# A graph network layer on one core: the vector engine's four products of a block in one run, the selection, the bases and the additions behind them

## The chip, the core and the metric

The kernel runs on one core of a Trainium2 chip. A core has a matrix engine (PE), a vector engine (DVE), a scalar engine (ACT), a general engine (POOL) and a sync engine (SP) that issues DMAs. Each works through its own instruction list in order, and they wait for one another on semaphores. The metric is the device time in microseconds (us) of one launch, the median of several runs.

## What is computed

A message passing layer over 12,500 nodes (128 features) and 412,500 edges that are sorted by their destination, with a residual addition and a layer norm behind it. Cut to what matters:

```
f0, f1   = node features @ W1            # 32 scalars, 32 vectors of 3
h        = gelu(gelu(edge_scalar_attr @ W_mlp1 / sqrt(8)) @ W_mlp2 / sqrt(64))
w00, w01, w10, w11 = h @ Wp_..           # 32 weights each, for every edge
e0, e1   = f0[edge_src], f1[edge_src]    # the gather
messages = w * e * edge_attr             # scalars and vectors, four kinds of product
n0, n1   = segment_sum(messages, edge_dst)
x        = layernorm(x + cos * self(x) + sin * (n0, n1) @ W2)
```

## The kernel before

A setup part builds a feature table in DRAM and the transposed accumulator `acc` in SBUF. The edge loop follows, then the layer norm. The edge loop is where the time is. It goes over 202 blocks of 2,048 edges; a block has 16 tiles of 128 edges, in four chunks of four tiles. The loop's body holds eight blocks (`RING`), one `step(b, ...)` each, and each engine has its own `step`. No scheduler sets the order: the program text of each engine is its order.

What a block needs, engine by engine:

- **POOL** gathers the rows of the feature table of 16 tiles with 16 indirect DMAs (L432) into one of four slots of `gath`. Before it gathers into a slot again it waits until the fourth products of the block four before are done (`s_prod[3]`).
- **PE** runs, for four blocks ahead, the two layers of the small network: layer 1 (L701) and layer 2 (L706), each in two halves, with the gelus of ACT (L513, L518) between them through one PSUM bank. So half 0 of layer 1, its gelu, half 0 of layer 2, its gelu, half 1 of layer 1, and so on form one serial chain. Between them it makes the block's weights, chunk by chunk (`radial`, L716), the segment sums of each chunk (L730), the transposes of these sums (L741) and the convolution with W2 (L749, `y_ps`).
- **DVE** makes the products of each chunk, weights times gathered rows (`products`, L958 once and L961 twice per chunk), the selection of the next block (`select`, L945 and L950: a one-hot by the destination, times the edge attributes), reads the window bases of the last block (`load_bases`, L974), and adds 16 windows of the last block's `y_ps` to `acc` (`add_windows`, L986).
- **ACT** runs the gelus, copies the sums and the transposed sums out of PSUM (L532, L539, L540), copies the indices of a later block (L497) and lays the next block's attributes in PSUM (L528), in the bank in which `y_ps` is too.

Waits that matter here: the products of chunk c wait for its weights (`s_w[c]`), its gathered rows and for PE's segment sum of the same chunk of the block before (`s_seg[c]`). The selection of block b+1 waits for `s_seg[3]` of block b-1 and for the attributes (`s_eap`). The convolution of block b-1 stands on PE in step b between the segment sum of chunk 1 and half 1 of layer 2. It waits for the transposed sums, for the additions of the block before (`s_add[15]`), and for the selection of block b+1 (`pe.wait_ge(s_sel, selected)`, with `selected = b + 2`), because the attributes in the same bank must have been read. The additions wait for the convolution (`s_y`).

## Time and profile before

| | us |
|---|---|
| median of three runs | 5436.78 |
| lowest and highest | 5435.55, 5450.42 |
| the profiled execution | 5456.17 |
| its span | 5454.4 |
| PE busy (matmul) | 3305.5 |
| POOL busy | 3103.3 |
| DVE busy | 1878.1 |
| ACT busy | 1180.1 |

The profiled execution is one of its own, 0.36% above the median. "Busy" counts computing instructions; a PE row's end is modelled, not observed. No engine is busy for more than 61% of the span, so the order of waits sets the time, not one engine's work. The rows further down say which waits ended what: in brackets behind a row stands the idle time of its engine before it, and what ended that.

### The profile page before, as it was taken

Reading aid. Unit: us, or ns where it says so; the run is one execution under the profiler, and the core shown is the slowest. Engines: PE = TensorE matmul, PEld = TensorE weight load, DVE = VectorE, ACT = ScalarE, POOL = GpSimd, SP = SyncE. Lnnn points to the kernel's source line nnn. Section 1 sums busy time; section 2 is a strip of 40 time slices with the busy share of each in tenths; the row PEclk is TensorE's granted clock in tenths of the full one; section 3 lists DMA queues with packets and bytes.
Section 4 is the critical chain, followed back from the end, with each engine's and each line's share of the span. In section 5 each row is a group of like instructions: output and inputs, shape, how many; then the busy total and the mean of one; then the engine's idle time right before and its main releaser. Section 6 shows DMA issues by size and latency. Waiting matters only on the chain.

```text
span 5454.4 us, 53973 instructions
## 1 busy us (share of the span) xinstructions
PE 3305.5 (61%) x15272; PEld 1812.2 (33%) x15272; DVE 1878.1 (34%) x6401; ACT 1180.1 (22%) x2646; POOL 3103.3 (57%) x3281
## 2 busy tenths in 40 slices
PE   5666656665665655666466666565665565666566
PEld 4233333332333323333233333233333333333334
DVE  2233333333333333333233333333333333333335
ACT  2122222221222212222122222121221221222124
POOL 5266566555665556556555665566566565566551
PEclk7677777777777777777777777777777777777777
DMA  6022222121221212212122222122122122222111
GB/s 151 16 46 46 44 46 45 45 44 41 46 46 43 45 41 46 46 43 46 44 42 45 45 46 44 42 47 46 42 46 46 43 46 44 45 46 46 44 44 59
DMA packets 586056, 256.03 MB, mean 47 GB/s; under 512 B 528383, under 2 KB 531867, under 8 KB 584347
## 3 DMA queue, kind: packets, MB, share of 16 engines
q0 software_dynamic: 103616, 211.52, 14.9%
q1 hardware_dynamic: 480572, 42.82, 6.7%
q14 instruction: 160, 1.31, 0.1%
q10 hardware_dynamic: 1696, 0.18, 0.0%
q8 instruction: 12, 0.20, 0.0%
HBM read 241.45 MB, written 12.81 MB: 47 GB/s over the span
## 4 chain that ended last, share of the span: by engine, by line
another core or an unknown queue 47%; PE 28%; issue 15%; ACT 8%; DVE 0%; ACTq 0%; DMA 0%; DVEq 0%; SPq 0%; POOL 0%; POOLq 0%
PE bank L706 7%; PE bank L716 5%; PE bank L701 5%; PE bank L749 5%; PE bank L730 3%; PE bank L741 2%; ACT h L513 2%; ACT big L518 1%; ACT ztsb L539 1%; ACT ztsb L540 1%; ACT bank L528 1%; PE bank L658 1%; ACT big L616 1%; ACT idx L497 1%
## 5 line engine op out<-in xcount | busy, mean ns | idle before, releaser
L432 POOL DMA_INDIRECT gath<-feature_table,idx x3224 | 3077.1, 954 | 2219.8 <-issue 1767.6
L716 PE MATMUL bank<-wpbd,big 128*128 128x256 f32 x3232 | 989.8, 436 | 98.4 <-issue 97.1
L958 DVE TENSOR_TENSOR big<-bank,gath 128x256 f32<-128x256 f32 x808 | 341.6, 423 | 1704.8 <-remote 1461.2
L716 PEld LDWEIGHTS bank<-wpbd,big 128*128 128x128 f32 x3232 | 711.8, 226 | 547.0 <-issue 480.0
L749 PE MATMUL bank<-ztsb,conv 128*128 128x128 f32 x1616 | 350.4, 384 | 788.8 <-ACT ztsb L540 491.2
L961 DVE TENSOR_TENSOR big<-bank,gath 128x384 f32<-128x384 f32 x1616 | 816.9, 547 | 0.0
L741 PE MATMUL bank<-ident,zsb 128*128 128x128 f32 x1616 | 340.1, 349 | 701.4 <-issue 544.6
L706 PE MATMUL bank<-h,w2bd 128*128 128x512 f32 x820 | 578.6, 795 | 259.8 <-ACT h L513 166.1
L986 DVE TENSOR_TENSOR acc<-acc,bank 128x8 f32 x3232 | 527.4, 163 | 598.5 <-remote 106.0
L701 PE MATMUL bank<-e8T,w1bd 128*128 128x512 f32 x820 | 591.9, 811 | 175.1 <-ACT big L518 90.2
L518 ACT ACTIVATE big<-bank 128x512 f32<-128x512 f32 x410 | 449.4, 1096 | 714.3 <-PE bank L706 396.7
L749 PEld LDWEIGHTS bank<-ztsb,conv 128*128 128x128 f32 x1616 | 298.8, 277 | 907.8 <-issue 503.9
L730 PE MATMUL bank<-big,sel 128*32 128x256 f32 x6464 | 596.3, 446 | 5.6 <-DVE big L961 4.9
L741 PEld LDWEIGHTS bank<-ident,zsb 128*128 128x128 f32 x1616 | 256.2, 182 | 963.4 <-issue 782.7
L532 ACT COPY zsb<-bank 128x512 f32<-128x512 f32 x404 | 237.9, 589 | 1106.1 <-remote 982.3
L945 DVE TENSOR_TENSOR sel<-rel_all,bank 128x128 f32<-128x128 f32 (+1 forms) x202 | 58.0, 287 | 1118.4 <-issue 952.0
L513 ACT ACTIVATE h<-bank 128x512 f32<-128x512 f32 x410 | 246.8, 602 | 796.7 <-remote 388.4
L539 ACT COPY ztsb<-bank 128x64 f32<-128x64 f32 x404 | 95.8, 237 | 1390.1 <-remote 1345.5
L701 PEld LDWEIGHTS bank<-e8T,w1bd 128*128 128x128 f32 x820 | 150.1, 229 | 410.8 <-issue 237.4
L706 PEld LDWEIGHTS bank<-h,w2bd 128*128 128x128 f32 x820 | 156.3, 237 | 373.8 <-ACT h L513 194.2
L730 PEld LDWEIGHTS bank<-big,sel 128*32 128x32 f32 x6464 | 136.3, 116 | 285.4 <-issue 285.2
L950 DVE TENSOR_TENSOR sel<-sel,bank 128x512 f32<-128x512 f32 x202 | 138.7, 686 | 6.9
(77 smaller groups left out, 756.2 us busy)
## 6 DMA issues: line engine op xcount, KB each, us to landing
gath<-feature_table,idx POOLq DMA_INDIRECT x3224
e<-in_edge_attr SPq DMA_DIRECT2D x416, 32.0 KB
ea_t<-in_edge_attr SPq DMA_DIRECT2D x100, 64.0 KB
feature_table<-gath SPq DMA_DIRECT2D x4, 1280.0 KB, 5.6
out<-big SPq DMA_DIRECT2D x4, 1280.0 KB
big<-in_x SPq DMA_DIRECT2D x3, 1280.0 KB, 8.5
dst_rows<-in_dst SPq DMA_DIRECT2D x1, 1536.0 KB
big<-in_src SPq DMA_DIRECT2D x1, 1408.0 KB
```

What stands on the lines that cost most here:

```text
L432: pool.indirect_dma_start(out=gath[:, s % SLOTS, t, :], out_offset=None, in_=table[:, :], in_offset=bass.IndirectOffsetOnAxis(ap=idx[:, s, ...
L513: act.activation(h1[:, h, :], hid_ps[:, :], ACT.Gelu_apprx_tanh, scale=1.0 / math.sqrt(RADIAL)).then_inc(s_h1[h], 1)
L518: act.activation(h2[:, m // SUPER % 2, :, :, 2 * (m % SUPER) + h], hid_ps[:, :].rearrange("q (b p) -> q b p", b=SUPER), ACT.Gelu_apprx_tan ...
L701: pe.matmul(hid_ps[:, :], w1bd[:, 2 * (m % SUPER) + h, :], e8T[:, :], start=True, stop=True)\
L706: pe.matmul(hid_ps[:, :], w2bd[:, :], h1[:, h, :], start=True, stop=True).then_inc(s_h2p[h], 1)
L716: last = pe.matmul(wgt_ps[c][:, 256 * r:256 * (r + 1)], h2[:, s // SUPER % 2, s % SUPER, 16 * g:16 * (g + 1), :].rearrange("q p a -> q (p ...
L730: last = pe.matmul(z_ps[32 * t:32 * (t + 1), c % 2, :], sel[:, s % 2, CT * c + t, :, :].rearrange("q k w -> q (k w)"), prod[:, c, t, :], s ...
L741: last = pe.transpose(zt_ps[:, h, c, :], zsb[:, c, 128 * h:128 * (h + 1)], ident[:, :])
L749: last = pe.matmul(y_ps, conv[:, k, :], ztsb[:, k, :], start=(k == 0), stop=(k == 3))
L958: dve.tensor_tensor(o[:, :, :, 0, :], w[:, :, :, 0, :], f[:, :, 0, :].unsqueeze(2).to_broadcast([128, n, 2, MUL]), ALU.mult)
L961: last = dve.tensor_tensor(o[:, :, h, 1:4, :], w[:, :, h, 1, :].unsqueeze(2).to_broadcast([128, n, 3, MUL]), f[:, :, 1:4, :], ALU.mult)
L986: dve.tensor_tensor(acc[:, at], acc[:, at], y_ps[:, WINDOW * t:WINDOW * (t + 1)], ALU.add)\
```

## The change

In DVE's `step` the selection of the next block stood between the products of chunk 1 and chunk 2, and the load of the bases between those of chunk 2 and chunk 3. Now the four products come first; the selection, the load and the additions follow them. Nothing else is touched, and no instruction is added or removed.

```diff
             def step(b, s, round_, first=False, last=False):
-                base = None
                 for c in range(CHUNKS):
-                    if c == 2 and not last:
-                        select(b + 1, s + 1, None if first else b)
-                    if c == 3 and not first:
-                        base = load_bases(b - 1)
                     products(b, s, c, round_ - (last and c < CUT_C), first)
+                if not last:
+                    select(b + 1, s + 1, None if first else b)
                 if not first:
-                    add_windows(b - 1, base)
+                    add_windows(b - 1, load_bases(b - 1))
```

DVE's list in one step of the loop, before. L958 opens the products of a chunk, L945 and L950 are the selection, L974 the load of the bases, L986 the first of the additions:

```order
L958 TENSOR_TENSOR big<-bank,gath 128x8x32 [waits segments_summed1,gathered3_1,radial_weights_done1]
L961 TENSOR_TENSOR big<-bank,gath 128x4x96 x2
L944 REGISTER_ALU [waits selection_ready,segments_summed3]
L945 ISA [waits attributes_in_psum]
L945 TENSOR_TENSOR sel<-rel_all,bank 128x128
L950 TENSOR_TENSOR sel<-sel,bank 128x512 [waits onehot_ready]
L958 TENSOR_TENSOR big<-bank,gath 128x8x32 [waits segments_summed2,gathered3_2,radial_weights_done2]
L961 TENSOR_TENSOR big<-bank,gath 128x4x96 x2
L974 ISA
L974 TENSOR_LOAD base_row
L958 TENSOR_TENSOR big<-bank,gath 128x8x32 [waits segments_summed3,gathered3_3,radial_weights_done3]
L961 TENSOR_TENSOR big<-bank,gath 128x4x96 x2
```

The same place of the same step, after:

```order
L958 TENSOR_TENSOR big<-bank,gath 128x8x32 [waits segments_summed1,gathered3_1,radial_weights_done1]
L961 TENSOR_TENSOR big<-bank,gath 128x4x96 x2
L958 TENSOR_TENSOR big<-bank,gath 128x8x32 [waits segments_summed2,gathered3_2,radial_weights_done2]
L961 TENSOR_TENSOR big<-bank,gath 128x4x96 x2
L958 TENSOR_TENSOR big<-bank,gath 128x8x32 [waits segments_summed3,gathered3_3,radial_weights_done3]
L961 TENSOR_TENSOR big<-bank,gath 128x4x96 x2
L944 REGISTER_ALU [waits selection_ready,segments_summed3]
L945 ISA [waits attributes_in_psum]
L945 TENSOR_TENSOR sel<-rel_all,bank 128x128
L950 TENSOR_TENSOR sel<-sel,bank 128x512 [waits onehot_ready]
L974 ISA
L974 TENSOR_LOAD base_row
L986 ISA [waits window_added15,conv_done]
```

The selection moved behind the last products, and the load of the bases stands right before the first wait of the additions.

PE's list is the same in both. The piece of it between the third weights and the second half of layer 2 (L730 segment sums, L701 layer 1, L716 weights, L749 convolution, L706 layer 2):

```order
L730 MATMUL bank<-big,sel 32x256 [waits products_ready0,sums_copied]
L730 MATMUL bank<-big,sel 32x256 x3
L701 MATMUL bank<-e8T,w1bd 128x512 [waits gelu2_done0]
L716 MATMUL bank<-wpbd,big 128x256 [waits products_ready3]
L730 MATMUL bank<-big,sel 32x256 [waits products_ready1]
L730 MATMUL bank<-big,sel 32x256 x3
L747 REGISTER_ALU [waits window_added15,transposed_sums_copied]
L749 MATMUL bank<-ztsb,conv 128x128 [waits selection_ready]
L749 MATMUL bank<-ztsb,conv 128x128 x3
L706 MATMUL bank<-h,w2bd 128x512 [waits gelu1_done1]
```

Nothing moved here; what moved is the place on DVE of the instruction that gives `selection_ready`.

## Rows read from the trace of the kernel before

**Rows 1.** The page: span, engines' busy time, share, instructions.

```profile
span 5454.4 us, 53973 instructions
PE 3305.5 (61%) x15272; PEld 1812.2 (33%) x15272; DVE 1878.1 (34%) x6401; ACT 1180.1 (22%) x2646; POOL 3103.3 (57%) x3281
```

**Rows 2.** Groups by line, 460 to 5300 us: count | busy, mean ns | idle before, releasers.

```profile
L432 POOL DMA_INDIRECT gath<-feature_table,idx x2995 | 2858.2, 954 | 1982.9 <-issue 1547.6 <-DVE big L961 435.3
...
L958 DVE TENSOR_TENSOR big<-bank,gath 128x256 f32<-128x256 f32 x747 | 315.9, 423 | 1601.3 <-remote 1380.8 <-issue 158.1 <-PE bank L716 58.6
```

**Rows 3.** Timeline, POOL: start, length, instruction [idle before <- what ended it].

```profile
2601.80 0.95 POOL L432 DMA_INDIRECT gath<-feature_table,idx  x1 [5.08 <-issue]
...
2620.69 0.95 POOL L432 DMA_INDIRECT gath<-feature_table,idx  x1 [0.30 <-issue]
2628.00 0.95 POOL L432 DMA_INDIRECT gath<-feature_table,idx  x1 [6.36 <-DVE big L961]
```

**Rows 4.** Timeline of the same block, other engines.

```profile
2599.28 2.07 PE L749 MATMUL bank<-ztsb,conv 128*128 128x128 f32 x8 [8.14 <-ACT ztsb L540]
...
2599.68 0.42 DVE L958 TENSOR_TENSOR big<-bank,gath 128x256 f32<-128x256 f32 x1 [5.15 <-remote]
...
2608.42 0.64 PE L730 MATMUL bank<-big,sel 128*32 128x256 f32 x8
2610.31 0.60 ACT L513 ACTIVATE h<-bank 128x512 f32<-128x512 f32 x1 [3.86 <-remote]
...
2611.92 1.03 PE L716 MATMUL bank<-wpbd,big 128*128 128x256 f32 x4
...
2618.82 0.58 ACT L532 COPY zsb<-bank 128x512 f32<-128x512 f32 x1 [7.91 <-remote]
...
2619.41 1.10 ACT L518 ACTIVATE big<-bank 128x512 f32<-128x512 f32 x1
...
2620.76 0.29 DVE L945 TENSOR_TENSOR sel<-rel_all,bank 128x128 f32<-128x128 f32 x1 [7.66 <-issue]
...
2621.09 0.69 DVE L950 TENSOR_TENSOR sel<-sel,bank 128x512 f32<-128x512 f32 x1
...
2624.51 0.42 DVE L958 TENSOR_TENSOR big<-bank,gath 128x256 f32<-128x256 f32 x1 [2.74 <-remote]
...
2625.05 1.16 PE L749 MATMUL bank<-ztsb,conv 128*128 128x128 f32 x8
...
2625.86 0.42 DVE L958 TENSOR_TENSOR big<-bank,gath 128x256 f32<-128x256 f32 x1
...
2626.20 1.01 DVE L961 TENSOR_TENSOR big<-bank,gath 128x384 f32<-128x384 f32 x2
...
2627.13 4.57 DVE L986 TENSOR_TENSOR acc<-acc,bank 128x8 f32 x16
```

**Rows 5.** Timeline of the next block: DVE's third and fourth products, and POOL's restart.

```profile
2636.55 0.43 DVE L958 TENSOR_TENSOR big<-bank,gath 128x256 f32<-128x256 f32 x1 [1.19 <-remote]
...
2650.62 0.42 DVE L958 TENSOR_TENSOR big<-bank,gath 128x256 f32<-128x256 f32 x1 [12.72 <-remote]
...
2652.75 0.95 POOL L432 DMA_INDIRECT gath<-feature_table,idx  x1 [4.89 <-DVE big L961]
```

**Rows 6.** Timeline of a long block, 2738 to 2767 us.

```profile
2738.56 0.95 POOL L432 DMA_INDIRECT gath<-feature_table,idx  x1 [19.82 <-issue]
...
2759.94 1.08 ACT L518 ACTIVATE big<-bank 128x512 f32<-128x512 f32 x1 [3.54 <-remote]
...
2761.07 2.08 PE L701 MATMUL bank<-e8T,w1bd 128*128 128x512 f32 x2 [2.60 <-ACT big L518]
...
2764.89 0.42 DVE L958 TENSOR_TENSOR big<-bank,gath 128x256 f32<-128x256 f32 x1 [1.34 <-PE bank L716]
...
2767.02 0.95 POOL L432 DMA_INDIRECT gath<-feature_table,idx  x1 [8.61 <-issue]
```

**Rows 7.** The load of the bases on DVE's sequencer: duration ns min/median/max.

```profile
L974 DVEq TENSOR_LOAD <-base_row x187: 1096/1100/1215, 461.2 to 5280.5; - x187
```

## The prediction

> **What bounds the kernel now.** I read four views: the page, the groups by line over the loop, POOL's timeline, and the timeline of all engines over one block. The page shows that no engine is full [rows 1]: PE has 61% and DVE 34%. DVE's own work can't be the limit, and what counts is where its instructions stand.
>
> The groups over 460 to 5300 us hold 2995 gathers, 187.2 blocks of 16, so a block takes 4840 / 187.2 = 25.86 us [rows 2]. POOL needs 0.95 + 0.31 us a gather, some 20 us, and waits for the rest.
>
> POOL's timeline shows a burst: its first gather starts at 2601.80, its last at 2620.69, and the next burst at 2628.00, released by DVE's L961 [rows 3]. That L961 belongs to the fourth products, which started at 2625.86 [rows 4]. In the next block they started at 2650.62 and POOL at 2652.75 [rows 5]. In both, POOL restarts 2.13 us behind the start of the fourth products. **The period of the loop is the distance from one start of the fourth products to the next.**
>
> What holds these products? Follow the block through [rows 4]. PE's segment sum L730 stands there from 2608.42 to 2609.06, but ACT's L532, which copies that sum, starts at 2618.82, with ACT idle before it: 9.8 us later. PE's weights L716 end at 2612.95 by their row, but the products that wait for them start at 2624.51, 11.6 us later. Half 0 of layer 1 is late too: ACT's L513 has waited 3.86 us at 2610.31. Then at 2624.5, 2.9 us behind POOL's last end (2621.64), all pending results of PE come out together: L958 at 2624.51, the convolution at 2625.05, L958 again at 2625.86. So PE's results arrive late from some 5 us into a burst on, and the rest come out in one release about 22.7 us after the burst's start (2624.5 - 2601.8). I call this the slow stretch. Why it exists the rows don't say. The Trainium skill says, in "Perfetto Trace Analysis", section "Tensor Engine Instruction", that the end of a PE instruction in a profile is computed from its size, and that the semaphore goes out only after PSUM has acknowledged. By the row's ends PE would be idle in the slow stretch, work that is shifted there would cost nothing, and the change would come to 0; by the rule PE's results are the late thing and there is no such slack. The waiters' starts above side with the rule.
>
> There are then three kinds of block:
> - (a) The third products are done before the release: 2636.55, and the fourth at 2650.62. The period is 2652.75 - 2628.00 = 24.75 us [rows 3, 5].
> - (b) The third products wait for the release too, and the fourth stand behind them, 1.35 us later (2624.51, 2625.86). The period is 2628.00 - 2601.80 = 26.20 us [rows 3, 4].
> - (c) The gelu behind layer 2, half 0, is held until near the release (ACT L518 at 2759.94 after 3.54 us). Then layer 1, half 1 (2761.07, 2.08 us), the fourth weights and the fourth products (2764.89) follow one after another in the open: 2767.02 - 2738.56 = 28.46 us [rows 6].
>
> The mean of 25.86 us lies between (a) and (b), with a few long ones.
>
> **The change, part by part.**
>
> *Third and fourth products ahead of the selection.* The selection takes 0.29 + 0.69 us, about 1.0 [rows 4]. It would be a gain if it held up the third products. It starts at 2620.76 and they start 3.75 us later, after 2.74 us of idle time that something else ended: the weights. On PE these weights stand behind layer 2, half 0, whose gelu (L518, 2619.41) precedes the attributes and the selection, so the selection is ready first. I take 0; the bounds are 0 and -1.0 us a block.
>
> *The load of the bases.* It takes 1.10 us on DVE's sequencer [rows 7], which runs ahead of the arithmetic; today that is beside the third products. Now it stands behind the selection and before the wait for the convolution. It can start when the selection's second part (0.69 us) is handed over, and the convolution needs another 1.16 to 2.07 us after that part ends [rows 4]: 1.10 against at least 1.85 us, so it is covered and costs 0. Without the cover it would be 1.1 us on the additions, not on POOL's restart.
>
> *The selection behind the fourth products.* This is the edit that costs. The convolution L749 waits for the selection of the next block. Now it starts 0.40 us before the fourth products (2599.28 against 2599.68) or 0.81 us before them (2625.05 against 2625.86) [rows 4]. After the change it can start only when the fourth products are through (1.35 us: 2626.20 + 1.01 - 2625.86) and the selection is (1.0 us): 2.35 us behind their start. So it moves 2.75 to 3.16 us later; I take 2.9. The price of this has two sides. On DVE the additions follow the convolution: they started at 2627.13, 1.27 us behind the start of the fourth products; now it is 2.35 + 1.16 = 3.5 us, and they take 4.57 us, so the next block's first products start 8.1 us behind, not 5.8. The first products are far from late in the slow stretch, and this alone costs 0. On PE, which works in order, half 1 of layer 2, the transposes, and the next block's weights, segment sums and layer 1 stand behind the convolution. They all move by 2.9 us, and since POOL restarts at the same distance from the fourth products as before, they move 2.9 us deeper into the burst, towards and into the slow stretch.
>
> *What of the 2.9 us reaches the period.* The lower end is 0: the release is set by POOL's burst, and what is pending comes out there anyway. The upper end by plain arithmetic is 2.9, if the chain through layers and gelus is serial all round. The kinds of block tell it better. With everything 2.9 us later no third products should be done before the release, so kind (a) goes: its blocks become (b), +1.45 us. And part of (b) becomes (c). In the block of rows 4 the layer-2 result arrived at 2619.4, 5.1 us before the release. A shift of 2.9 us that is stretched on the way, as every result in the slow stretch takes several times its row's length (L532 9.8 us behind a 0.64 us group), can use that up. I put 4 blocks in 10 in (c). That is the weakest step, and its ends, none and all, bound the rest.
>
> **The sum.** 0.6 x 26.20 + 0.4 x 28.46 = 27.10 us. The present mean has, beside its three kinds, rare long stops; the one ahead of rows 6 kept POOL idle for 19.82 us where 6 are usual. Four or five such over 187 blocks are 0.3 us a block, and they stay. So 27.4 against 25.86, about +1.57 us, over 200 blocks +315 us. The setup and the norm are untouched. On the profiled execution (5456.17) that gives 5770; on the median, which is 0.36% lower, 5436.78 + 315 = 5750 us. With all blocks in (b): 26.5, +0.64 x 200 = +130, 5565 us. With all in (c): 28.8, +2.9 x 200 = +580, 6020 us.
>
> **The rivals.**
> - *Absorbed.* The shifted PE work lands in the first 5 us of the burst, where results still come in time, and few blocks change their kind. For it: the release depends on POOL alone. Against it: at 2610.31 a result is 3.86 us late already [rows 4], and that is the chain that is shifted. 5420 to 5565 us.
> - *Faster.* The third products are freed from the selection in time and all blocks are of kind (a). One mechanism: in blocks where the weights come early, DVE sits before the selection (7.66 us in rows 4) and the third products could already run. The point is whether chunk 2's weights come before the selection. In the next block they started at 2636.55 with only 1.19 us of idle before them, so there are such blocks, but the release keeps the fourth back all the same. It pays only where the third products are still behind at the release. Then 24.75 + 0.3 = 25.05 us, -0.8 x 200 = -160: 5275 us.
> - *Worse than all (c).* The gelu of layer 1 is held until the release too; then layer 2, about as long as layer 1's 2.08 us, stands in the open too [rows 6]: 28.8 + 2.1 = 30.9 us a block, +5.0 x 200 = +1000, 6440 us if all blocks did so.
>
> **Chances.** My forecast, 5565 to 6020 us: 0.60. Absorbed: 0.17, about half of it within 0.3%. Faster: 0.15. Worse: 0.08. The range 5420 to 6080 holds the first two and slivers of the others, about 0.8. A measurement of this kernel can tell some 0.3% (16 us) from no change. Faster by more than that 0.15, within it 0.08, slower 0.77.
>
> **What would show it.** POOL's period in the groups by line: 27.4 us, so some 176 blocks in 4840 us. The convolution L749 starts about 2.35 us behind the start of the fourth products in every block, and DVE's additions never before 3.5. The third products start at the release, with the fourth 1.35 us behind them in nearly all blocks. DVE's busy time stays at 1878 us. ACT's L518 shows more and longer waits right before the release. I am wrong if the third products still finish well before the fourth in half of the blocks (absorbed), if POOL's idle time per block falls (faster), or if the period grows while the distance between POOL's last gather and the fourth products stays at 3 us, since then the burst itself is slower and PE is not the cause.

## The result: slower by a seventh, twice as much as forecast

| | before | changed |
|---|---|---|
| median of four runs, us | 5436.16 | 6204.44 |
| lowest and highest | 5432.37, 5450.42 | 6184.29, 6218.24 |
| profiled execution | 5456.17 | 6218.24 |

The ratio is 1.1415, with an interval of 1.1378 to 1.1451. That is +768 us where +315 was forecast, and beyond the upper end of the range (6080). The sign and the edit that costs hold; the size and the mix of blocks don't.

The page of the changed kernel, which answers to [rows 1]:

```profile
span 6216.4 us, 53973 instructions
PE 3592.9 (58%) x15272; PEld 1925.2 (31%) x15272; DVE 1879.6 (30%) x6401; ACT 1190.4 (19%) x2646; POOL 3112.3 (50%) x3281
```

DVE does the same work in the same time (1879.6 against 1878.1 us). PE's rows are longer by 287 us at the same count; its mean granted clock is 0.72, against 0.76 before. The groups by line, 460 to 5300 us, of the changed kernel (count | busy, mean ns | idle before, releasers), which answer to [rows 2]:

```profile
L432 POOL DMA_INDIRECT gath<-feature_table,idx x2612 | 2499.9, 957 | 2334.5 <-issue 1758.7 <-DVE big L961 575.8
...
L749 PE MATMUL bank<-ztsb,conv 128*128 128x128 f32 x1304 | 252.8, 355 | 344.3 <-DVE sel L950 344.3
...
L532 ACT COPY zsb<-bank 128x512 f32<-128x512 f32 x327 | 191.8, 586 | 1631.5 <-remote 1419.6 <-PE bank L730 211.8
```

2612 gathers are 163.25 blocks: 4840 / 163.25 = 29.65 us a block, against 25.86. The difference of 3.8 us over 200 blocks is 760 us, so the loop holds the whole loss. A gather takes 957 ns against 954; what grew is POOL's idle time. Two rows of before, from the same view, show who waits for what now:

```profile
L749 PE MATMUL bank<-ztsb,conv 128*128 128x128 f32 x1496 | 326.2, 386 | 737.1 <-ACT ztsb L540 456.7 <-issue 280.4
...
L532 ACT COPY zsb<-bank 128x512 f32<-128x512 f32 x373 | 219.8, 589 | 1030.2 <-remote 919.3 <-PE bank L730 61.4 <-issue 49.2
```

Before, the selection doesn't appear among the releasers of the convolution L749: 456.7 us of its idle time end with ACT's copy L540, and 280.4 the profile ties to nothing. Now L950, the selection, is the only releaser, with 344.3 / 163 = 2.1 us a block. And ACT's copy of the sums, L532, waits 1631.5 / 327 = 5.0 us a time and not 1030.2 / 373 = 2.8, nearly all of it "remote", which stands for a release that the profile can't tie to a row: PE's rows had long ended by their modelled ends.

One block of the changed kernel, on the timeline (start, length, engine, instruction [idle before <- what ended it]); it answers to [rows 3 to 5]:

```profile
2990.48 0.96 POOL L432 DMA_INDIRECT gath<-feature_table,idx  x1 [10.81 <-DVE big L961]
...
2996.22 1.12 PE L701 MATMUL bank<-e8T,w1bd 128*128 128x512 f32 x2
...
2997.23 0.42 DVE L958 TENSOR_TENSOR big<-bank,gath 128x256 f32<-128x256 f32 x1
...
3001.79 0.60 ACT L513 ACTIVATE h<-bank 128x512 f32<-128x512 f32 x1 [6.19 <-remote]
...
3002.44 2.07 PE L706 MATMUL bank<-h,w2bd 128*128 128x512 f32 x2 [3.67 <-issue]
...
3005.32 0.42 DVE L958 TENSOR_TENSOR big<-bank,gath 128x256 f32<-128x256 f32 x1 [6.74 <-remote]
...
3012.38 0.59 ACT L532 COPY zsb<-bank 128x512 f32<-128x512 f32 x1 [9.99 <-remote]
...
3013.01 1.11 PE L741 MATMUL bank<-ident,zsb 128*128 128x128 f32 x4 [6.79 <-ACT zsb L532]
3013.11 1.11 ACT L518 ACTIVATE big<-bank 128x512 f32<-128x512 f32 x1
3013.17 0.42 DVE L958 TENSOR_TENSOR big<-bank,gath 128x256 f32<-128x256 f32 x1 [6.49 <-remote]
...
3014.06 1.08 PE L730 MATMUL bank<-big,sel 128*32 128x256 f32 x8
...
3015.07 2.08 PE L701 MATMUL bank<-e8T,w1bd 128*128 128x512 f32 x2
...
3016.94 1.73 PE L716 MATMUL bank<-wpbd,big 128*128 128x256 f32 x4
...
3018.71 0.43 DVE L958 TENSOR_TENSOR big<-bank,gath 128x256 f32<-128x256 f32 x1 [4.19 <-PE bank L716]
...
3020.29 0.69 DVE L950 TENSOR_TENSOR sel<-sel,bank 128x512 f32<-128x512 f32 x1
3020.85 0.96 POOL L432 DMA_INDIRECT gath<-feature_table,idx  x1 [10.48 <-DVE big L961]
...
3021.13 1.45 PE L749 MATMUL bank<-ztsb,conv 128*128 128x128 f32 x8 [1.88 <-DVE sel L950]
...
3022.71 4.59 DVE L986 TENSOR_TENSOR acc<-acc,bank 128x8 f32 x16 [1.73 <-PE bank L749]
```

Read it in this order:
- POOL restarts at 3020.85, 2.14 us behind the fourth products (3018.71), as before. From burst to burst it is 30.37 us, and POOL stood still for 10.48 of them.
- The convolution starts 2.42 us behind the fourth products (3021.13), not 0.4 to 0.8 ahead of them.
- Layer 1, half 0, ends by its row at 2997.34, and ACT starts its gelu at 3001.79, 11.3 us into the burst; in [rows 4] it was 8.5 (2610.31 - 2601.80). So the result is 2.8 us later, but its row on PE only 1.0: it starts 5.74 us into the burst, and 4.70 in the block of [rows 4], whose line is below. The rest is lateness that grew.
- The gelu of layer 2 (L518) starts at 3013.11, 22.6 us into the burst, together with the third products (3013.17, 22.7 us in) and the copy of the sums. In [rows 4] it was out 17.6 us into the burst. Between these two blocks a shift of 2.8 us has become one of 5.0 and has hit the release.
- Behind the release stand, on PE, one after another: transposes, a segment sum, layer 1's half 1, the fourth weights. The fourth products come 5.54 us behind the third, not 1.35.
- DVE isn't what holds them. Its first products start at 2997.23, right behind the additions; then it stands idle for 6.74 us before the second (3005.32). In 170 of the 178 blocks counted below it waits more than 1 us there, 7.3 in the median, so the later additions and first products cost nothing there.

The row of layer 1, half 0, in the block of [rows 4]:

```profile
2606.50 1.13 PE L701 MATMUL bank<-e8T,w1bd 128*128 128x512 f32 x2
```

How PE ran there, from the stretches of the changed kernel (us, then busy us of PE, PEld, DVE, ACT, POOL, then the granted clock, DMA share, GB/s):

```profile
3012.30:3019.00 6.70, 5.99 (x26) 2.93 (x26) 1.64 (x4) 2.87 (x7) 0.00 (x0) 0.55 0.37 18
...
3027.00:3032.00 5.00, 4.07 (x20) 1.97 (x18) 2.23 (x7) 0.60 (x1) 3.78 (x5) 1.00 0.20 54
```

Behind the release PE was granted 0.55 of its clock, mostly the lower level of 1.2 GHz; layer 1 takes 2.08 us there and 1.12 at the full clock. The lower level didn't begin with the release: layer 2 already took 2.07 us at 3002.44, after 3.67 us without work, and the clock stayed at 0.50 from there on while PE stood still. So the row of work that now stands in the open also runs at its slowest.

One block is no mean, so I took all blocks from the 20th to the 198th in both traces. Medians of the start, in us behind the first gather of the block's burst:

| | before | changed |
|---|---|---|
| PE's row of layer 1, half 0 (L701) | 3.5 | 5.7 |
| its gelu on ACT (L513) | 4.9 | 12.0 |
| the gelu of layer 2, half 0 (L518) | 12.1 | 23.2 |
| third products | 19.1 | 22.7 |
| fourth products | 23.5 | 28.4 |

A row on PE that moved by 2.2 us gives a result that comes 7 us later, and the next layer's comes 11 us later. Before, layer 1's result was at its reader 0.04 us behind the row's end in the median; in the changed kernel it is 5.2 us behind it.

Sorted into the kinds of the prediction, (c) if the gelu of layer 2, half 0, starts more than 21 us into the burst, (b) if only the third products start later than 21.5, (a) otherwise:

| kind | before: blocks, mean period | changed: blocks, mean period |
|---|---|---|
| (a) | 111, 25.0 us | 5, 25.4 us |
| (b) | 57, 26.1 us | 27, 26.8 us |
| (c) | 10, 34.4 us | 146, 30.4 us |

Of the ten (c) before, four hold the long stops of over 40 us; the other six take 28.46 to 30.91 us, 29.5 in the mean. The changed mix gives (5 x 25.4 + 27 x 26.8 + 146 x 30.4) / 178 = 29.7 us, near the measured 29.65. The convolution stands 2.3 to 2.4 us behind the fourth products in every block. POOL's burst has kept its length (19.84 and 19.88 us from first gather to last end), and its gap went from 5.6 to 10.65 us, all medians.

### The profile page after: what moved, and what is told of

It reads as the page before. It is cut to its first block, busy times and chain, and to the rows that moved or that the text cites. A ratio compares the mean times of both kernels' runs of the same rounds, so it can differ in the third digit from the quotient of the medians.

```text
span 6216.4 us, 53973 instructions
## 1 busy us (share of the span) xinstructions
PE 3592.9 (58%) x15272; PEld 1925.2 (31%) x15272; DVE 1879.6 (30%) x6401; ACT 1190.4 (19%) x2646; POOL 3112.3 (50%) x3281
## 4 chain that ended last, share of the span: by engine, by line
another core or an unknown queue 44%; PE 29%; issue 15%; ACT 6%; DVE 5%; DVEq 0%; ACTq 0%; DMA 0%; POOL 0%; POOLq 0%
PE bank L701 7%; PE bank L716 6%; PE bank L706 4%; PE bank L730 4%; PE bank L741 3%; PE bank L749 3%; DVE big L961 2%; ACT zsb L532 2%; ACT h L513 2%; DVE sel L950 1%; PE bank L658 1%; ACT big L518 1%; ACT ztsb L539 1%; ACT big L616 1%
## 5 line engine op out<-in xcount | busy, mean ns | idle before, releaser
L958 DVE TENSOR_TENSOR big<-bank,gath 128x256 f32<-128x256 f32 x808 | 343.0, 424 | 3360.4 <-remote 2516.0
L706 PE MATMUL bank<-h,w2bd 128*128 128x512 f32 x820 | 710.4, 964 | 800.0 <-issue 629.5
L716 PE MATMUL bank<-wpbd,big 128*128 128x256 f32 x3232 | 1083.8, 469 | 32.1 <-issue 30.8
L741 PE MATMUL bank<-ident,zsb 128*128 128x128 f32 x1616 | 378.6, 379 | 1159.6 <-ACT zsb L532 797.3
L716 PEld LDWEIGHTS bank<-wpbd,big 128*128 128x128 f32 x3232 | 792.7, 251 | 601.1 <-issue 518.4
L986 DVE TENSOR_TENSOR acc<-acc,bank 128x8 f32 x3232 | 529.7, 164 | 772.3 <-PE bank L749 346.4
L741 PEld LDWEIGHTS bank<-ident,zsb 128*128 128x128 f32 x1616 | 285.7, 201 | 1475.5 <-ACT zsb L532 892.7
L701 PE MATMUL bank<-e8T,w1bd 128*128 128x512 f32 x820 | 648.3, 883 | 87.1 <-issue 42.6
L518 ACT ACTIVATE big<-bank 128x512 f32<-128x512 f32 x410 | 451.7, 1102 | 970.1 <-PE bank L706 447.1
L730 PE MATMUL bank<-big,sel 128*32 128x256 f32 x6464 | 613.3, 457 | 0.0
L532 ACT COPY zsb<-bank 128x512 f32<-128x512 f32 x404 | 236.9, 586 | 1962.7 <-remote 1698.5
L513 ACT ACTIVATE h<-bank 128x512 f32<-128x512 f32 x410 | 245.2, 598 | 1688.7 <-remote 1178.5
L749 PE MATMUL bank<-ztsb,conv 128*128 128x128 f32 x1616 | 313.5, 355 | 428.0 <-DVE sel L950 425.9
L706 PEld LDWEIGHTS bank<-h,w2bd 128*128 128x128 f32 x820 | 186.9, 282 | 907.7 <-issue 709.9
L749 PEld LDWEIGHTS bank<-ztsb,conv 128*128 128x128 f32 x1616 | 264.9, 248 | 534.9 <-issue 397.2
L701 PEld LDWEIGHTS bank<-e8T,w1bd 128*128 128x128 f32 x820 | 162.6, 248 | 342.9 <-issue 231.3
L730 PEld LDWEIGHTS bank<-big,sel 128*32 128x32 f32 x6464 | 137.9, 117 | 281.0 <-issue 280.8
L950 DVE TENSOR_TENSOR sel<-sel,bank 128x512 f32<-128x512 f32 x202 | 138.8, 687 | 7.0
L540 ACT COPY ztsb<-bank 128x192 f32<-128x192 f32 x404 | 130.4, 323 | 0.0
```

The costliest lines, as they stand in the source:

```text
L513: act.activation(h1[:, h, :], hid_ps[:, :], ACT.Gelu_apprx_tanh, scale=1.0 / math.sqrt(RADIAL)).then_inc(s_h1[h], 1)
L518: act.activation(h2[:, m // SUPER % 2, :, :, 2 * (m % SUPER) + h], hid_ps[:, :].rearrange("q (b p) -> q b p", b=SUPER), ACT.Gelu_apprx_tan ...
L532: act.copy(zsb[:, :, :], z_ps).then_inc(s_zc, 1)
L701: pe.matmul(hid_ps[:, :], w1bd[:, 2 * (m % SUPER) + h, :], e8T[:, :], start=True, stop=True)\
L706: pe.matmul(hid_ps[:, :], w2bd[:, :], h1[:, h, :], start=True, stop=True).then_inc(s_h2p[h], 1)
L716: last = pe.matmul(wgt_ps[c][:, 256 * r:256 * (r + 1)], h2[:, s // SUPER % 2, s % SUPER, 16 * g:16 * (g + 1), :].rearrange("q p a -> q (p ...
```

## The experiments

The theory: the selection now comes late, it holds the convolution, PE works in order, and what stands behind the convolution arrives later. The rivals: DVE's own order costs it (products and additions later in the row, called A in the expectations); the load of the bases; the place of layer 1's half 1 ahead of the fourth weights.

### The changed kernel again

No edit.

> The changed kernel itself once more, beside the kernel before. In the four runs so far the kernel before took 4224 us, not 5436: there PE's results came in time, POOL never waited (20.2 us a block, its own 16 gathers) and no edit moved the time. Theory (the change puts more on PE's chain, and that costs only where PE's results are late): where the kernel before takes 4224 us, this one takes 4224 us too, within 0.3%; where it takes 5436 us, some 6200 us. Rival A (the cost is DVE's order itself): slower than before in both, by some 2 us a block or 9%.

6315.6 us against 5564.53 for the kernel before beside it, ratio 1.1364 (1.1270 to 1.1457). Its groups, 460 to 4000 us:

```profile
L432 POOL DMA_INDIRECT gath<-feature_table,idx x1876 | 1795.5, 957 | 1744.5 <-issue 1301.6 <-DVE big L961 442.9
```

3540 us / (1876 / 16) = 30.2 us a block. The loss stands in a second place where PE's results come late; both kernels are 2% longer there, so I take it for another chip than the first, though the first one's number isn't on record. The kinds are the same: 163 of 178 blocks are (c), with layer 2's gelu at 23.4 us in the median.

### Single steps, with all gathers

Convolution moved behind layer 2 in the changed kernel:

```diff
                 segment_sum(b, s, 1)
-                if not first:
-                    convolve(b - 1, BLOCKS if last else b + 2)
                 if not last:
                     layer2(b + SUPER, 1)
+                if not first:
+                    convolve(b - 1, BLOCKS if last else b + 2)
```

> The changed kernel with one edit on PE: the convolution stands behind half 1 of layer 2 instead of ahead of it (still ahead of the transposes). Theory (PE's layers and gelus stand behind a convolution that now waits for the selection behind the fourth products): half 1 of layer 2 and its gelu no longer wait, the transposes and the next layer 1 still do, so a part comes back: a period of some 28 us, about 5850 us (5650 to 6050). Rival A (the cost is on DVE: the additions and the next block's first products start 2.5 us later): the additions start as late as before this edit or later, so 6200 us or more. Rival B (the products themselves are slower or POOL's burst is): 6200 us.

The kernel before, whose convolution also waits for the fourth products; DVE's order is untouched:

```diff
+                if products is not None:
+                    pe.wait_ge(s_prod[CHUNKS - 1], products)
                 pe.wait_ge(s_add[TILES - 1], b + 1)
...
-                    convolve(b - 1, BLOCKS if last else b + 2)
+                    convolve(b - 1, BLOCKS if last else b + 2, b + 1)
```

> The kernel before, DVE's order untouched, with one wait more on PE: the convolution also waits for the fourth products of the running block, which puts its start 1.35 us behind their start, where the median was 0.4 us ahead of it. Theory: the delay of the convolution alone makes most of the loss, here with a shift of 1.8 us in place of 2.8: 5800 us (5600 to 6100), with blocks in which layer 2 comes only at the release. Rival A (order on DVE): the additions move by only some 1.3 us and the four products stay as they were, so at most 5470 us.

The kernel before with only the load of the bases moved:

```diff
-                    if c == 3 and not first:
-                        base = load_bases(b - 1)
...
-                    add_windows(b - 1, base)
+                    add_windows(b - 1, load_bases(b - 1))
```

> The kernel before with the smallest part of the change alone: the load of the bases stands behind the fourth products, the selection stays where it was. Theory: the load is no cause; the additions may start up to 1.1 us later, which reaches neither PE's chain nor POOL: 5437 us, within 0.3%. Rival C (the load on DVE's sequencer is on the path): 1.1 us a block, 5650 us.

The changed kernel with the fourth weights ahead of layer 1, half 1:

```diff
                 segment_sum(b, s, 0, first)
+                radial(b, s, 3, first)
                 if not last:
                     pe.wait_ge(s_h2[0], b + (SUPER + 1))
                     layer1(s, 1)
-                radial(b, s, 3, first)
```

> The changed kernel with one edit on PE: the fourth weights stand ahead of half 1 of layer 1, so they no longer wait for the gelu behind layer 2. Theory (after the release the fourth products wait for gelu, layer 1 and weights in a row): that row is cut, the fourth products follow the third at the release, and the period falls to some 26.2 to 27.5 us: 5600 us (5480 to 5800). Rival A (the additions and first products on DVE): the first products come as late as before the edit, so 6200 us.

All four ran on one chip, on which the kernel before takes 4223.72 us and not 5436:

| edit | us | ratio | interval |
|---|---|---|---|
| convolution behind layer 2 (changed) | 4226.16 | 1.0006 | 0.9996 to 1.0015 |
| convolution waits for products (before) | 4225.30 | 1.0004 | 0.9994 to 1.0013 |
| load of the bases alone (before) | 4224.64 | 1.0002 | 0.9992 to 1.0012 |
| fourth weights ahead (changed) | 4225.90 | 1.0004 | 0.9994 to 1.0014 |

None moves the time, and as tests of the cause they failed: this chip lacks what the theory is about. The timeline of the kernel with the load moved:

```profile
2002.36 0.64 PE L730 MATMUL bank<-big,sel 128*32 128x256 f32 x8 [2.61 <-DVE big L961]
...
2003.07 0.59 ACT L532 COPY zsb<-bank 128x512 f32<-128x512 f32 x1 [3.54 <-PE bank L730]
```

L532 starts 0.07 us behind the modelled end of the segment sum. In [rows 4] it was 9.8 us. There is no slow stretch here, with POOL in the same burst. So POOL never stops; the groups, 460 to 4000 us, of that kernel and then of the changed one with its convolution behind layer 2:

```profile
L432 POOL DMA_INDIRECT gath<-feature_table,idx x2805 | 2684.9, 957 | 855.4 <-issue 852.7 <-ACT idx L497 2.7
...
L749 PE MATMUL bank<-ztsb,conv 128*128 128x128 f32 x1400 | 236.9, 321 | 37.7 <-DVE sel L950 34.1 <-issue 2.9
```

```profile
L432 POOL DMA_INDIRECT gath<-feature_table,idx x2805 | 2684.8, 957 | 855.4 <-issue 855.4
...
L749 PE MATMUL bank<-ztsb,conv 128*128 128x128 f32 x1400 | 359.1, 438 | 1003.3 <-DVE sel L950 997.0 <-issue 6.2
```

In both POOL takes (2684.9 + 855.4) / 2805 = 1.262 us a gather, 20.2 us a block, and waits for nothing but its own issue. In the second, PE stands still for 1003.3 / 175 = 5.7 us a block before the convolution, for the selection, and it costs nothing: POOL is the bound and PE has room. The unedited changed kernel was not run on such a chip with all gathers; two of these kernels hold it with one step of PE moved.

Two of these kernels ran seven more times, on chips where the kernel before takes 4215 to 4217 us:

> The changed kernel with the fourth weights ahead of half 1 of layer 1 on PE (the same kernel as in the run where the kernel before took 4224 us; this is told where it takes 5400 or more). Theory (late results of PE come out at the release, and then gelu, half 1 of layer 1 and the fourth weights follow in a row before the fourth products): that row is cut and the block falls from 30 to some 26.5 us: a ratio of 1.03 to the kernel before (1.00 to 1.06). Rival A (DVE's late additions and first products are the cost): the ratio stays at 1.14. On a chip where the kernel before takes 4224 us both say 1.00.

4217.88 us against 4215.27, ratio 1.0006 (0.9997 to 1.0016).

> The kernel before with DVE's order untouched and a convolution that also waits for the running block's fourth products. Theory: the later convolution is what puts PE's layers into the stretch of late results: a ratio of 1.07 (1.03 to 1.13), and ACT's gelu behind layer 2 (half 0) near the release in most blocks. Rival A (DVE's order): 1.00 to 1.01. On a chip where the kernel before takes 4224 us both say 1.00.

4217.81 us, ratio 1.0007 (0.9998 to 1.0017).

> The kernel before, DVE's order untouched, with a convolution that also waits for the running block's fourth products; a third try, since both earlier ones stood beside a kernel before of some 4220 us, where nothing waits for PE. Theory: where the kernel before takes 5400 us or more, a ratio of 1.07 (1.03 to 1.13). Rival A (DVE's order): 1.00 to 1.01. Where it takes 4220 us both say 1.00.

4218.08 us against 4215.99, ratio 1.0004 (0.9995 to 1.0014).

> The changed kernel with all gathers and the fourth weights ahead of half 1 of layer 1 on PE, once more. Theory, where the kernel before takes 5400 us or more: a ratio of 1.03 (1.00 to 1.06), as the row of gelu, layer 1 and weights behind the release is cut. Rival A: 1.14. Where the kernel before takes 4220 us: 1.00.

4217.83 us against 4216.84, ratio 1.0003 (0.9993 to 1.0013).

> The kernel before with a convolution that also waits for the running block's fourth products. Theory: where the kernel before takes 5400 us or more, a ratio of 1.07 (1.03 to 1.13), since 1.4 of the 2.4 us are added to PE's chain. Rival A (DVE's order): 1.00 to 1.01. Where the kernel before takes 4220 us: 1.00.

4219.86 us against 4216.34, ratio 1.0008 (0.9996 to 1.0019).

> The changed kernel with the fourth weights ahead of half 1 of layer 1. Theory, where the kernel before takes 5400 us or more: with half the gathers this gave back 0.9 us a block of 2.0 on the chain; behind the release it also takes layer 1 out of the row before the fourth products, 4 us of 30: a ratio of 1.03 (1.00 to 1.08), against 1.14 without it. Rival A: 1.14. Where the kernel before takes 4220 us: 1.00.

4218.02 us, ratio 1.0002 (0.9991 to 1.0013).

> The changed kernel with the fourth weights ahead of half 1 of layer 1, in the hope of a chip where the kernel before takes 5400 us or more. Theory there: a ratio of 1.03 (1.00 to 1.08), against 1.14 without the edit; Rival A: 1.14. Where the kernel before takes 4220 us: 1.00.

4216.41 us against 4215.47, ratio 1.0004 (0.9993 to 1.0016).

The kernel before with the same step, the fourth weights ahead of layer 1's half 1:

> The kernel before with the fourth weights ahead of half 1 of layer 1 on PE. Theory: in the blocks whose layer 2 comes at the release the fourth products no longer wait for it, and elsewhere they follow the release as before: a gain of 0.3 to 1.0 us a block, a ratio of 0.97 (0.95 to 1.00). Rival A says nothing of it: 1.00.

4215.46 us against 4215.27, ratio 0.9999 (0.9989 to 1.0008). None of the edited kernels met a chip where PE's results come late.

### With POOL out of the way: half of the gathers

If POOL hides the loss on these chips, it should show with a shorter burst. These kernels leave out every second gather and zero the tiles that it would have filled, so that DVE and PE do the same work (what they return is no longer the layer's result):

```diff
-                for t in range(CT * c, CT * (c + 1)):
+                for t in range(CT * c, CT * (c + 1), 2):
...
-                dve.wait_ge(s_g[m % SLOTS][c], round_ * (16 * CT) + 16 * CT)
+                dve.wait_ge(s_g[m % SLOTS][c], round_ * (8 * CT) + 8 * CT)
```

The changed kernel with this edit:

> The changed kernel with every second gather of a tile left out (8 per block, the other tiles' rows stay zero), all else the same, so POOL's burst is 10 us long. Theory (the late results belong to POOL's burst and come out 3 us behind its last gather): the release falls some 13 us behind the start of the burst, the fourth products follow 5 us later and the period is 19 to 21 us: about 4200 us. Rival D (PE is late for a reason of its own, and POOL only waits): the release stays some 22 us behind and the time stays over 5500 us.

3139.97 us (3138.24 to 3141.71). Both expectations were missed, 4200 us and over 5500. Both took the slow stretch for given, and this chip has none, so whether the late results belong to POOL's burst stays untested.

The kernel before with this edit:

> The kernel before with every second gather left out (8 per block, the other tiles' rows stay zero), so that POOL is out of the way and the engines' own chain sets the period on any chip. The changed kernel with the same cut took 3140 us, with a chain of weights, fourth products, selection, convolution and PE in every block. Theory (in the changed kernel PE stands still from the fourth weights to the end of the selection, 2.4 us, before it goes on with the convolution and the layers): here PE doesn't, 2.0 to 2.5 us a block less, 2700 us (2620 to 2800). Rival A (the changed order on DVE itself): DVE has 1857 us of work in 3140 us, and the two orders would differ by at most 1 us a block: 2940 us or more.

2711.81 us (2710.61 to 2714.02), as expected. It and the two that follow ran on a second such chip; the kernel before with all gathers takes 4216.84 us there and 4215.27 beside the changed one above, so the two chips are taken as equal. So with half the gathers the change costs 428 us, (3139.97 - 2711.81) / 202 = 2.12 us a block, where with all of them on such chips nothing was measured. The chain of waits (start, us, what), of the kernel before with half the gathers:

```profile
1502.29 0.57 PE bank L733 x8
1502.85 1.09 PE bank L752 x8
1503.94 0.86 PE bank L709 x2
```

and of the changed one (line numbers are three higher: L719 weights, L733 segment sum, L752 convolution, L709 layer 2, L964 products, L948 and L953 selection):

```profile
1513.39 0.88 PE bank L719 x4
1514.63 1.01 DVE big L964 x2
1515.65 0.20 DVE sel L948
1515.88 0.70 DVE sel L953
1516.58 0.14 issue
1516.71 1.13 PE bank L752 x8
1517.84 0.86 PE bank L709 x2
```

Before, the chain is PE alone, segment sum, convolution, layer 2 without a gap. Changed, it leaves PE at the fourth weights, goes through the fourth products and the selection on DVE, and comes back at the convolution. That is the mechanism of the theory, from the rows: 1516.71 - 1513.39 - 0.88 = 2.44 us in which no PE row is on the chain. A segment sum of 0.57 us, which was on the chain before, now runs beside it, so 1.87 us are left as loss. The groups, 460 to 2460 us, before and changed, say the same of all blocks:

```profile
L752 PE MATMUL bank<-ztsb,conv 128*128 128x128 f32 x1296 | 187.7, 288 | 0.0
```

```profile
L752 PE MATMUL bank<-ztsb,conv 128*128 128x128 f32 x1104 | 169.0, 300 | 256.0 <-DVE sel L953 256.0
```

PE stands still 256.0 / 138 = 1.86 us a block for the selection (8 rows each), of 2.12 that the change costs.

Is it the convolution's wait, or DVE's order? The kernel before with half the gathers and the convolution's extra wait for the fourth products:

> The kernel before with every second gather left out, and a convolution that also waits for the running block's fourth products. DVE's order is that of before. Theory: PE stands still for the fourth products (1.4 us) in every block, but not for the selection: 1.4 us of the 2.4, so between the two orders: 2950 us (2850 to 3020). Rival A (DVE's order): as the kernel before with half the gathers.

2928.84 us, as expected: (2928.84 - 2711.81) / 202 = 1.07 us a block, half of the loss, with DVE in its old order. Its chain:

```profile
1509.32 0.57 PE bank L733 x8
1509.89 0.92 issue
1510.81 1.13 PE bank L754 x8
```

The 0.92 us of "issue" is the wait for the fourth products: on the timeline these end at 1510.71, and the convolution starts at 1510.81. The group of the same kernel, 460 to 2460 us:

```profile
L754 PE MATMUL bank<-ztsb,conv 128*128 128x128 f32 x1190 | 168.9, 285 | 149.8 <-issue 149.8
```

That is 149.8 / 149 = 1.0 us a block of 1.07. Rival A, by which this kernel takes what the kernel before takes, falls here. In the changed kernel the selection (0.20 + 0.70 + 0.14 = 1.04 us) comes on top. This second half is read from one block's chain and has no run of its own; 1.07 + 1.04 = 2.11 agrees with the whole of 2.12, and by the idle time alone (0.92 + 1.04 = 1.96) some 0.15 us could still be something else, DVE's order among it.

Does the wait for the fourth products hang on layer 1, half 1, which stands ahead of their weights? The changed kernel with half the gathers and the fourth weights ahead of it:

> The changed kernel with every second gather left out and the fourth weights ahead of half 1 of layer 1 on PE. Theory: the fourth products and the selection now run beside layer 1, the segment sum of chunk 1 and so on (1.06 + 0.57 us of PE work), so only 0.8 us a block of the 2.4 are left: 2800 us (2700 to 2900), against 3140 without this edit. Rival A: 3140 us, within 2%.

2935.34 us, outside of 2700 to 2900: 204.63 us or 1.01 a block come back, about one layer 1 (1.06), and the rest, (2935.34 - 2711.81) / 202 = 1.11 us, stays. Its chain:

```profile
1509.74 1.07 PE bank L719 x4
1511.18 1.01 DVE big L964 x2
...
1513.26 1.13 PE bank L752 x8
```

From the weights' end to the convolution it is 2.45 us, as in the changed kernel (2.44); layer 1 now runs beside that, and only its length comes back. I had counted on more.

### A version meant to be faster than both

The kernel before, the fourth weights ahead of layer 1's half 1, and POOL waiting for each chunk's products and not for the fourth:

```diff
-                    if free is not None:
-                        pool.wait_ge(s_prod[CHUNKS - 1], free)
-                        pool.sem_inc(s_round, 1)
                     for c in chunks:
+                        if free is not None:
+                            pool.wait_ge(s_prod[c], free)
+                            pool.sem_inc(s_round, 1)
                         gather(s, c)
```

> A version meant to be faster than both: the kernel before with the fourth weights ahead of half 1 of layer 1, and POOL's gathers of chunk c waiting for the products of chunk c of four blocks before, in place of the fourth products for all. Theory: where the kernel before takes 5400 us or more, POOL no longer waits for the release before a block's first gathers, a ratio of 0.93 (0.80 to 1.02; its burst becomes longer, and with it the stretch in which results are late may). Where the kernel before takes 4220 us, POOL never waits, and the ratio is 1.00.

4206.65 us against 4215.47, ratio 0.9979 (0.9968 to 0.9990), again on a chip without the slow stretch. These 9 us aren't gained in the steady loop. The groups of the first 460 us, of the kernel before with the fourth weights ahead alone, and of this one:

```profile
L432 POOL DMA_INDIRECT gath<-feature_table,idx x295 | 281.8, 955 | 122.1 <-issue 121.8 <-ACT idx L497 0.3
```

```profile
L432 POOL DMA_INDIRECT gath<-feature_table,idx x303 | 289.3, 955 | 114.6 <-issue 114.0 <-DVE big L961 0.6
```

It is eight gathers ahead at 460 us, 8 x 1.26 = 10 us, and keeps them: between 460 and 4000 us both issue 2812. On a chip with the slow stretch POOL could start on chunks 0 to 2 of the next block earlier; what that is worth was not measured.

## Why the prediction was wrong in its size

**Right: the bound.** The period is the distance of the fourth products, and POOL restarts 2.1 us behind them in both kernels. POOL's burst did not change.

**Right: the edit that costs, and its first size.** The convolution was put at 2.35 us behind the fourth products and came at 2.3 to 2.4 in every block; before, it stood 0.40 us ahead of them in the median. The row of layer 1 on PE moved by 2.2 us. With half the gathers, on a chip without the slow stretch, the shift is on PE's chain alone: 1.07 us of it by a run, 1.04 read from rows.

**Right: what costs nothing.** The load alone gave 1.0002; that was measured where POOL is the bound, so it shows less than it seems. With half the gathers the wait for the products and the selection come close to the whole, and no load is on the chain.

**Wrong: how many blocks turn long.** The step that failed is "kind (a) goes: its blocks become (b)", with 4 blocks in 10 in (c). 146 of 178 are (c), and before only 67 were (b) or (c) together, so most of (a) went straight to (c). The 5.1 us of room that I took from [rows 4] belong to a block in which layer 2's gelu was late already, at 17.6 us. The median block had it at 12.1, some 10.6 us ahead of the release, and that room was used up too. What I mis-sized is the stretching. I carried the shift on as 2.9 us with a little on top. Measured, 2.2 us on PE's row became 7 at layer 1's gelu and 11 at layer 2's, as the row now ends behind the first 5 us of the burst, in which results still came on time (last section).

The signs that I gave could not tell this apart. "With the fourth 1.35 us behind them in nearly all blocks" was itself at odds with 4 in 10 of kind (c), and less than 3 us came in 25 of 178 (77 before). The sign of *absorbed*, third products well ahead of the fourth in half of the blocks, showed in the other 153, with nothing absorbed.

In numbers: with 0.82 in (c) and the rest as predicted the sum is 0.18 x 26.20 + 0.82 x 28.46 + 0.3 = 28.4 us instead of 27.4: of the 453 us that I was short, this step is some 190.

**Wrong: how long such a block is.** I took 28.46 us from one block [rows 6]. The same trace held five more without a stop, and that one was the shortest; the mean of the six is 29.5. In [rows 6] the gelu of layer 2 came out at 2759.94, 21.4 us into the burst, ahead of the release that the other blocks have at 22.7. And between that gelu and the fourth products stood 4.95 us; in the changed block it is 5.60, as the transposes and a segment sum come out in the same release and go first. The changed kernel's (c) takes 30.4 us, 2.0 more than [rows 6]; over 0.82 x 200 blocks that is some 320 us.

**Wrong: the long stops.** "They stay" put 0.3 us a block on top. Before has 4 periods of over 32 us among those 178, the changed kernel none. That took 60 us off. The three together: 190 + 320 - 60 = 450, against 453 missing.

**The upper bound.** "All in (c)", 28.8 us, bounded a share but not the length of (c), and one long block was taken for the longest. The rival beyond it (30.9 us, a further result in the open) had 0.08. Its time a block was near the 30.4 us of kind (c), its mechanism was another: layer 1's gelu was held past 21 us in none of the 178 blocks, and what stands in the open is what goes ahead of the fourth weights.

**A reading to correct.** The third products at 2624.51 start 11.6 us behind the end of their weights' row, but not all of that is a late result: DVE's own selection stood between and ended at 2621.78. The 9.8 us of ACT's copy L532 has no such row between.

**What was not asked: whether the slow stretch belongs to the kernel.** "Why it exists the rows don't say" stood there, and the sum took it as given. In the two places where the kernel before takes 5436 and 5565 us it is there, and the change costs 14%. On the four other chips that ran it is not, and kernels with the change and one step moved cost nothing that could be measured.

What stays open: why PE's results are late on some chips, and, since no edited kernel met one, whether there the convolution's wait alone brings the whole 3.8 us. The shift at layer 1, its stretching and the row behind the release are read from the traces of the two kernels; the runs show the chain only where results are prompt, where it is worth 2.1 us.

## What to carry over

An instruction that moves nowhere near the bottleneck engine is dear if an in-order engine waits for it: ask who holds the semaphore's other end, and what stands behind that wait in the same list. When results are released in one batch, price a delay by what then stands in a row behind the release, at the clock granted there, and not by the delay. And take the room and the length of a kind of block from many of them: the one at hand for the room was late already, and the one for the length was the shortest of six.

## What the runs showed of the hardware

The kernel before takes 5436 and 5565 us in two places and 4215 to 4224 on four other chips. A gather takes the same time on all (954 to 957 ns). What differs is when PE's results reach the engine that waits: 0.07 us behind the row's modelled end in the kernel with the load moved, 9.8 us in [rows 4], with POOL's indirect DMAs issuing in both. Late results come out about 22.7 us after the burst's first gather, 2.9 us behind its last. What makes a chip do so, no run shows; nor was any chip seen in both conditions.

It is PE's results that are late, not every wait. In the same stretch of [rows 4], in which ACT's copy came 9.8 us behind PE's row, DVE's selection (L945, 2620.76) started 0.15 us behind the end of ACT's copy on which it waits, with POOL still issuing:

```profile
2620.28 0.33 ACT L528 COPY bank<-ea_t 128x64 f32<-128x64 f32 x1
```

Over the whole trace of before it is 0.15 us in the median of 189 such waits, and PE's transposes start 0.05 us behind ACT's copy of the sums.

How late depends on where in the burst PE's row ends (medians, counted as above). Before, layer 1's rows that end less than 5 us into the burst have their gelu 0.04 us behind them (110 rows), layer 2's that end at 6.5 to 7 us have it 5.3 us behind, and at 8 to 10 us 8.2. In the changed kernel layer 1's rows that end at 6.5 to 7 us, 108 of 178, have it 5.2 us behind. Single blocks lie up to some 4 us off these medians, and why it grows is not shown.

The mean granted clock goes with it: 0.76 and 0.72 (before and changed) where results are late, 0.87 to 0.88 for the kernel before and 0.84 for those with the later convolution where they are prompt, and 0.96 to 0.98 in the kernels with half the gathers, where PE hardly stands still. Within a block of the changed kernel it was 0.50 in the long wait, 0.55 behind it and 1.00 some 8 us later.
